# Weight splits of two experts moved into the phase before, and a product kept in PSUM, in a four-stage transformer kernel

## The reference, cut to what matters

```python
scores = softmax(x2d @ wg_router.T)                  # 32 experts
topk_w, topk_idx = top_k(scores, 6)
xe = zeros((E, C, D)).at[flat_idx, safe_pos].add(x_rep)   # C = 384 slots for an expert
g, u = xe @ w_gate, xe @ w_up                        # width 176
ye = (silu(g) * u) @ w_down
y = sum over the 6 choices of ye * topk_w
sh = silu(x2d @ ws_gate) * (x2d @ ws_up) @ ws_down   # shared experts, width 352
out = x + y + sh                                     # x2d is the layer-normed x
```

## Time and profile before

| | us |
|---|---|
| three runs: median (lowest to highest) | 1120.21 (1117.7 to 1127.51) |
| profiled execution, its own time | 1119.49 |
| its span | 1117.7 |
| mean granted TensorE clock | 0.975 |
| PE busy | 1031.1 (92%) |
| DVE busy | 758.2 (68%) |
| ACT busy | 600.6 (54%) |
| POOL busy | 563.0 (50%) |

### The profile page before, as it was taken

One profiled execution on the slowest core, in us unless ns is written; L12 is line 12 of the kernel. 1 busy time (PEld: TensorE's weight loads), 2 busy tenths in 40 slices (PEclk: granted clock), 3 DMA queues, 4 the chain that ended last, 5 costly groups with the idle time before them and its releaser, 6 DMA issues. The chain is left out here.

```text
span 1117.7 us, 16700 instructions
## 1 busy us (share of the span) xinstructions
PE 1031.1 (92%) x6084; PEld 865.8 (77%) x6084; DVE 758.2 (68%) x1344; ACT 600.6 (54%) x1060; POOL 563.0 (50%) x411
## 2 busy tenths in 40 slices
PE   5899999999999999999998899996978887999992
PEld 4788888888888888888886676654765686999992
DVE  4877764777557776567775644467688755888877
ACT  3566663666536666456662423333523245888871
POOL 1574633756236563365540357762224777655553
PEclk9999999999999999999999999999998898999996
DMA  7510340003701991000001146631300366777766
GB/s 202 50 34 1 48 47 1 24 1 44 52 1 38 230 216 45 1 1 1 1 1 39 44 161 204 218 132 57 109 2 5 108 224 231 232 231 227 234 206 225
DMA packets 45343, 109.79 MB, mean 98 GB/s; under 512 B 8487, under 2 KB 25525, under 8 KB 43216
## 3 DMA queue, kind: packets, MB, share of 16 engines
q1 hardware_dynamic: 38352, 95.46, 32.5%
q0 software_dynamic: 6912, 13.30, 3.2%
HBM read 94.27 MB, written 41.29 MB: 121 GB/s over the span
## 5 line engine op out<-in xcount | busy, mean ns | idle before, releaser
L460 POOL TENSOR_TENSOR at_prob<-at_prob,at_inv_sum 128x1024 f32<-128x1024 f32 x128 | 243.8, 1907 | 272.7 <-DVE at_inv_sum L678 272.7
L641 ACT ACTIVATE at_pt_h<-ps 128x512 fp32r<-128x512 f32 x256 | 139.2, 596 | 139.4 <-PE ps L566 139.3
L729 DVE TENSOR_TENSOR at_pt_l<-ps,at_pt_h 128x512 fp32r<-128x512 f32 x256 | 164.4, 684 | 60.9 <-ACT at_pt_h L641 60.9
L718 DVE TENSOR_REDUCE at_neg_max<-ps 128x1 f32<-128x1024 f32 x128 | 154.6, 1208 | 35.8 <-PE ps L41 35.4
L608 ACT ACTIVATE at_prob<-ps,at_neg_max 128x1024 f32<-128x1024 f32 x128 | 143.7, 1123 | 15.3 <-DVE at_neg_max L718 15.3
L566 PE MATMUL ps<-ident,at_prob 128*128 128x128 f32 x1024 | 133.4, 273 | 5.1 <-POOL at_prob L460 3.9
L566 PEld LDWEIGHTS ps<-ident,at_prob 128*128 128x128 f32 x1024 | 118.9, 140 | 23.0 <-POOL at_prob L460 4.7
L2111 POOL DMA_INDIRECT lines<-f_y,f_x_raw x96 | 96.0, 1000 | 72.1 <-ACT f_y L2027 42.6
L39 PE MATMUL ps<-at_k_h,at_q_h 128*128 128x512 f32 x256 | 108.4, 423 | 0.0
L39 PE MATMUL ps<-at_pt_h,at_v_h 128*128 128x512 f32 x256 | 100.3, 392 | 0.0
L40 PE MATMUL ps<-at_k_l,at_q_h 128*128 128x512 f32 x256 | 100.2, 391 | 0.0
(11 more groups left out here) (318 smaller groups left out, 2456.5 us busy)
## 6 DMA issues: line engine op xcount, KB each, us to landing
e_raw<-in_we SPq DMA_DIRECT2D x32, 624.0 KB, 4.3
f_cw_row<-cw SPq DMA_DIRECT2D x32, 512.0 KB, 4.2
slots<-in_empty SPq DMA_DIRECT2D x4, 3456.0 KB, 41.9
f_x_raw<-slots SPq DMA_DIRECT2D x32, 432.0 KB, 4.9
lines<-in_empty SPq DMA_DIRECT2D x3, 2048.0 KB, 33.3
f_e_raw<-in_we SPq DMA_DIRECT2D x32, 128.0 KB, 2.5
at_wq_raw<-in_wq SPq DMA_DIRECT2D x4, 512.0 KB, 3.6
at_wo_raw<-in_wo SPq DMA_DIRECT2D x4, 512.0 KB, 3.5
```

What stands on the lines that cost most here:

```text
L460: nc.gpsimd.tensor_tensor(prob[:, t % RING, :], prob[:, t % RING, :], inv_sum[:, t:t + 1].broadcast_to([P, T]), ALU.mult).then_inc(normed, 1)
L641: nc.scalar.activation(pt_h[:, e[1] % PT, :], turned(e[1]), ACT.Copy).then_inc(pt_high, 1)
L718: nc.vector.tensor_reduce(neg_max[:, t:t + 1], slot(n, start), AX.XY, ALU.max, negate=True).then_inc(maxed, 1)
L729: nc.vector.tensor_tensor(pt_l[:, e[1] % PT, :], turned(e[1]), pt_h[:, e[1] % PT, :].bitcast(F32), ALU.subtract).then_inc(pt_split, 1)
```

## The change

1. The tiles `e_h` and `e_l` and their two semaphores are made outside the silu experts' phase, so that the linear attention can write them (`e_h1`, `e_l1`, `e_high1`, `e_split1`).
2. ScalarE's copies for experts 0 and 1 move into the linear attention, ahead of `square(6)`. GpSimd's subtractions for experts 0 and 1 move there too, behind a wait for the last state update and ahead of `shared_l`.
3. In the head of the silu experts ScalarE and GpSimd split expert 2 instead of 0 and 1. The expert loop no longer splits expert 2.
4. SyncE's order becomes weights 3, weights 4, slots 0, slots 1, slots 2, weights 5, slots 3, weights 6, and so on: `load_weights(n + 3)` stands behind `load_slots(n)`, where `load_weights(n + 2)` stood.
5. The shared experts' product is written back over the up projection in PSUM; `s_act` is gone. `s_h` and `s_l` are made from PSUM. The up projection alternates between banks 4, 5 and banks 6, 7.

```diff
@@ linear attention, GpSimd @@
+                pool.wait_ge(state_done, TT)
+                for n in range(AHEAD1):
+                    pool.wait_ge(net.e_high1, n + 1)
+                    nc.gpsimd.tensor_tensor(net.e_l1[:, n, :], net.e_raw1[:, n, :], net.e_h1[:, n, :].bitcast(F32),
+                                            ALU.subtract).then_inc(net.e_split1, 1)
                 pool.wait_ge(chain, NB * ROOT)
@@ linear attention, ScalarE @@
+                for n in range(AHEAD1):
+                    act_e.wait_ge(net.e_loaded1[n], 16)
+                    nc.scalar.activation(net.e_h1[:, n, :], net.e_raw1[:, n, :], ACT.Copy).then_inc(net.e_high1, 1)
                 for i in range(TT - 2, TT):
                     square(i)
@@ constants @@
+WRING1 = 4
+AHEAD1 = 2
@@ silu experts, SyncE @@
+                for n in range(AHEAD1):
+                    load_weights(n + RAW)
                 load_slots(0)
                 load_slots(1)
-                for n in range(1, EXP1):
-                    if n > 1:
-                        load_slots(n)
-                    if n + RAW - 1 < EXP1:
-                        load_weights(n + RAW - 1)
+                for n in range(2, EXP1):
+                    load_slots(n)
+                    if n + RAW < EXP1:
+                        load_weights(n + RAW)
@@ TensorE @@
+        def s_banks(k):
+            return slice(4 + 2 * (k % 2), 6 + 2 * (k % 2))
                     project(2, k, rows, SG)
-                    if k:
-                        pe.wait_ge(timed, k)
-                        project(4, k, rows, SU)
-                    else:
+                    if k == 0:
                         ranks(1)
                         norm.wait_parts(pe)
-                        project(4, k, rows, SU)
+                    if k >= 2:
+                        pe.wait_ge(act_split, k - 1)
+                    project(s_banks(k).start, k, rows, SU)
@@ ScalarE @@
-                for n in range(2):
-                    high_weights(n)
+                high_weights(AHEAD1)
-                    nc.scalar.activation(s_h[0:rows, k, :], s_act[0:rows, k % 2, :], ACT.Copy).then_inc(act_high, 1)
+                    nc.scalar.activation(blocks(s_h[0:rows, k, :]), ps[0:rows, s_banks(k), :], ACT.Copy).then_inc(act_high, 1)
-                    if n + 2 < EXP1:
+                    if AHEAD1 < n + 2 < EXP1:
                         high_weights(n + 2)
@@ GpSimd @@
-                for n in range(2):
-                    pool.wait_ge(e_high, n + 1)
-                    nc.gpsimd.tensor_tensor(e_l[:, n % WRING, :], e_raw[:, n % RAW, :], e_h[:, n % WRING, :].bitcast(F32),
-                                            ALU.subtract).then_inc(e_split, 1)
+                pool.wait_ge(e_high, AHEAD1 + 1)
+                nc.gpsimd.tensor_tensor(e_l[:, AHEAD1, :], e_raw[:, AHEAD1, :], e_h[:, AHEAD1, :].bitcast(F32),
+                                        ALU.subtract).then_inc(e_split, 1)
@@ VectorE @@
-                    if k >= 2:
-                        dve.wait_ge(act_split, k - 1)
-                    nc.vector.tensor_tensor(blocks(s_act[0:rows, k % 2, :]), ps[0:rows, 4:6, :], blocks(s_silu[0:rows, k % 2, :]),
+                    nc.vector.tensor_tensor(ps[0:rows, s_banks(k), :], ps[0:rows, s_banks(k), :], blocks(s_silu[0:rows, k % 2, :]),
                                             ALU.mult).then_inc(timed, 1)
-                    nc.vector.tensor_tensor(s_l[0:rows, k, :], s_act[0:rows, k % 2, :], s_h[0:rows, k, :].bitcast(F32),
-                                            ALU.subtract).then_inc(act_split, 1)
+                    nc.vector.tensor_tensor(blocks(s_l[0:rows, k, :]), ps[0:rows, s_banks(k), :],
+                                            blocks(s_h[0:rows, k, :].bitcast(F32)), ALU.subtract).then_inc(act_split, 1)
-                    if n == 1:
-                        dve.wait_ge(e_split, 2)
-                    if 2 <= n + 1 < EXP1:
+                    if n == AHEAD1:
+                        dve.wait_ge(e_split, AHEAD1 + 1)
+                    if AHEAD1 < n + 1 < EXP1:
                         low_weights(n + 1)
```

More of the change, by code:

```diff
@@ L1693, in silu_experts_phase @@
 def silu_experts_phase(nc, net, out):
-    WRING, XRING, YRING = 4, 7, 6
+    WRING, XRING, YRING = WRING1, 7, 6
     SENT = 8 - TOP1
@@ L1712, in silu_experts_phase @@
         row = sb("row", [P, TT, ROW1])
-        e_h, e_l = sb("e_h", [P, WRING, W1E], F32R), sb("e_l", [P, WRING, W1E], F32R)
+        e_h, e_l = net.e_h1, net.e_l1
         x_raw = sb("x_raw", [P, XRING, SLOTS, ROW1])
@@ L1725, in silu_experts_phase @@
         e_raw, e_loaded, RAW = net.e_raw1, net.e_loaded1, RAW1E
-        s_silu, s_act = only_early("s_silu", [P, 2, T]), only_early("s_act", [P, 2, T])
+        s_silu = only_early("s_silu", [P, 2, T])
         s_h, s_l = only_early("s_h", [P, SH1, T], F32R), only_early("s_l", [P, SH1, T], F32R)
@@ L1754, in silu_experts_phase @@
         x_loaded = [sem(f"x_loaded{r}") for r in range(XRING)]
-        e_high, e_split = sem("e_high"), sem("e_split")
+        e_high, e_split = net.e_high1, net.e_split1
         x_turned, x_high, x_split = sem("x_turned"), sem("x_high"), sem("x_split")
@@ L2305, in program @@
         net.e_raw1 = sb("e_raw1", [P, RAW1E, W1E])
+        net.e_h1, net.e_l1 = sb("e_h1", [P, WRING1, W1E], F32R), sb("e_l1", [P, WRING1, W1E], F32R)
+        net.e_high1, net.e_split1 = (ctx.enter_context(nc.semaphore(n)) for n in ("e_high1", "e_split1"))
         net.shared1_high, net.shared1_split = (ctx.enter_context(nc.semaphore(n)) for n in ("shared1_high", "shared1_split"))
```

## The result

The changed kernel takes 1144.64 us (median of 4 runs, 1137.29 to 1145.85) where the kernel before takes 1121.74 (4 runs): a ratio of 1.0186, 95% interval 1.0142 to 1.0229. It is slower, by about 21 to 23 us. The forecast was 1138, with a range of 1129 to 1148.

What follows compares the result with a forecast made beforehand. The prediction took the loop to be bound by TensorE. The turn of expert 29 moves from 1072.38 to 945.2 + 11 x 13.27 = 1091.2, so +18.8 on the profiled 1119.49: 1138 us, range 1129 to 1148.

Steps and rivals of the forecast that it cites:

- The deciding step: SyncE's queue in the expert loop: gathered rows released one expert later, 3.24 us before use against a median 5.3 us transfer.
- the round: Expert loop: two iterations take 7.52 + 0.41 + 5.3 + 0.04 = 13.27 us instead of 11.18, eleven times.
- the landing: Expert loop: time for gathered rows to arrive after issue, taken as the median 5.3 us, mean allowed 4.9 to 5.8.
- The head: Silu experts before the loop: 6.0 us gained (4 to 7), all eaten by the turn of expert 7.
- The copy: Head: VectorE's 128x24 copy, held by GpSimd's subtractions, drops from 2.38 to 0.20 us, gaining 2.18.
- the 1.25 for expert 2's low parts: Head: the dispatch at 910.67, which took 2.23 us beside expert 2's low parts, becomes 1.25 us shorter.
- The 2.75 beside `s_low`: Head: three GpSimd dispatches beside `s_low` return to 0.98 us, saving 1.04 + 1.00 + 0.71.
- The size in the loop: From the turn of expert 7 at 945.2 to that of 29 at 1091.2: 11 rounds of 13.27 us.
- the fall of the clock: Rival for the whole loop: TensorE's idling lowers its clock; at half clock 1225 us in all; chance 0.03.
- The tail: What follows the turn of expert 29 was claimed to keep its length.
- Costed at nothing: Moved splits hide in ScalarE's and GpSimd's idle time; the product written to PSUM costs at most 0.1 us each.
- The Trainium skill's fit: DMA estimate: rows land in 3.0 us alone, 4.1 behind weights, giving the landings-of-about-4.1 rival, 1124 us, chance 0.07.

Runs made afterwards that it cites:

- Experiment 2: Kernel before with SyncE's new order alone; weights still split in the head, product still in SBUF: 1147.68 us, ratio 1.0257.
- experiment 1: Changed kernel with slots n + 1 again ahead of weights n + 3 in SyncE's queue: 1116.39 us, ratio to before 0.9965; second series 1116.0 us, 0.9956.
- experiments 3 and 4: For 3 see experiment 3; 4: changed kernel loading only half of each expert's weights from expert 6 on, order as changed: 1132.72 us, ratio to before 1.0114.
- experiment 3: Changed kernel, same wait for expert n's low parts, but slots n + 1 issued ahead of weights n + 3: 1118.8 us, ratio to before 0.9989.
- experiment 5: Changed kernel with gathered rows again one expert further ahead and the shared experts' product back in SBUF: 1120.42 us, ratio to before 0.9988.
- experiment 6: Kernel before with the shared experts' product in PSUM alone, head splits and SyncE's order as before: 1120.83 us, ratio 1.001.

## Why the prediction was right

**The deciding step, SyncE's order**, held in every part. The turn before which the wait sits, the round and its terms are in the chain after: 1004.56 to 1009.86 is landing plus 0.04, 1009.86 to 1017.47 is 7.61 (forecast 7.52), 0.38 for the issue. Experiment 2 shows that the order alone makes the loss, experiment 1 that nothing else in the change does, experiments 3 and 4 that its size goes by the landing.

**The head** held nearly to the figure. The copy: 0.18 for 2.38. Dispatches began 2.7 us earlier (868.01 to 865.28), of which 0.5 is the block's earlier start. The turn of 4 came at 923.90 (forecast 924.4), that of 5 at 933.83 (933.6), that of 7 at 944.64 (945.2). The sum behind it was mis-sized in one term: 3.4 us less from the first to the fortieth dispatch (55.2 to 51.8) instead of 4.0. Nothing was got of the 1.25 for expert 2's low parts: the dispatch at 913.24 met those of expert 3 instead and took 2.25. The 2.75 beside `s_low` were got in full. The rest of the 3.4 is luck: another dispatch, that of 917.22, had been long before (1.65), was not in the forecast, and has no counterpart after.

**The size in the loop** was short by 3.8 us. The forecast had 146.0 for eleven rounds; from 944.64 to 1094.48 are 149.84, or 13.62 a round. The mis-sized term is the landing. The forecast took the median of 5.3 for each; the ten on the chain of the loop have a mean of 5.5, which makes 2.0. Eight of them landed in 4.7 to 5.3, and the rounds in which the chain comes straight back took 12.75 to 13.55, as forecast. Two took 15.1 and 15.4, with loads that landed in 7.1 and 7.4 us. Such loads are not new. One mark of the first is a slow issue by SyncE, and before the change there were slow issues too (from the two timelines, before and after):

```profile
1013.04 1.91 SPq L1853 DMA_DIRECT2D f_x_raw<-slots  x1
...
1017.85 1.54 SPq L1866 DMA_DIRECT2D f_x_raw<-slots  x1
```

The load of 1013.04 landed in 6.0 us, and one of 1029.86, issued in 1.64, in 6.8; neither held anyone, as there were 8.8 us of slack. What makes an issue slow no run shows. Behind the turn of 1024.99, ahead of which TensorE had stood still for 2.99 us, the granted clock fell: it is 0.52 from 1024.99 to 1031.30, transposes took 1.54 instead of 0.87, and the next turn came 8.6 us later. This iteration and a later one, both of which the chain crosses on TensorE, took 14.4 together where the forecast has 13.3 for two. I had given the fall of the clock 0.03 as a state of the whole loop; it came as an episode. In the window 949 to 1072 the clock is still 0.97. The last 0.7 of the 3.8 are the other terms of the round, 8.04 on average for 7.97.

**The tail** kept its length only nearly: from the turn of 29 to the end 47.5 us, before 45.3. The turn of 30 came 7.4 behind that of 29, at a lowered clock (0.65 from 1094.48 to 1099.20; three loads of rows had gone out together, the first landing in 7.4 us). The account closes: the forecast's 18.8, less 0.6 for the better head, plus 3.8 for the loop and 2.2 for the tail is 24.2, and the spans differ by 24.3. But for the 0.6 the misses have one sign, so the forecast of 1138 was not saved by errors that cancel; it was 6.6 short of 1144.64.

**Costed at nothing**: the moved splits were hidden (ScalarE 828.85 to 831.2, GpSimd 833.12 to 838.8, VectorE's roots from 839.07 on at their 0.23 to 0.29). The product written to PSUM took 1.22 to 1.23, no more than the 1.21 to 1.23 to SBUF.

**The Trainium skill's fit** for a DMA ("DMA: Bandwidth & Descriptors", section "Anatomy of one DMA — SWDGE (gpsimd) path", made on DMAs that GpSimd issues) gives, as an estimate, 4.1 us for the rows behind the weights and 3.0 for the rows alone. For these loads, which SyncE issues, the traces do not agree: the median is 5.0 with the weights just ahead, and 3.5 with the weights behind them in experiment 3.

What stays open: the moves alone (experiment 5, 0.9988) and the PSUM product alone (experiment 6, 1.001) show no gain outside their intervals, the two together 4 to 5 us. Each of the two figures is uncertain by some 2 us either way, so it is not shown that the sum is more than its parts; nor is it shown how the 4 to 5 us divide between the moves and the product.

## What to carry to other kernels

In a queue that is served in order, a wait is paid by whatever stands behind it. When a load is moved in such a list, count for each entry how many iterations ahead of its use it is now released, and set that lead against the time to landing with what goes out in front of it. Here the lead went from 8.8 to 3.2 us against a landing of 5. The queue's waits for the low parts of the weights add up to 100.9 us before and to 100.0 in experiment 3, and do little or no harm in either. The same 24 waits with the entries behind them shifted by one cost 2%, and come to 141.4 us because the loop is longer. The sum of the waits is no measure of what they cost; the slack of what stands behind them is.

## What the runs showed of the hardware

One thing I had not expected is how much the same kernel's head moves from run to run. Experiment 1's kernel began its dispatches at 864.19 us in one profiled execution and at 873.81 in the other, spans 1112.4 and 1119.8. The same two windows of both, the faster one first, with the granted clock behind the busy times:

```profile
615.00:650.00 35.00, 30.05 (x169) 25.60 (x169) 21.49 (x102) 15.66 (x19) 11.66 (x6) 0.95 0.26 97
...
780.00:850.00 70.00, 60.08 (x655) 45.17 (x656) 53.52 (x111) 26.38 (x54) 25.51 (x26) 0.98 0.12 44
```

```profile
615.00:650.00 35.00, 30.42 (x138) 25.96 (x138) 21.03 (x101) 14.32 (x17) 9.97 (x6) 0.79 0.22 69
...
780.00:850.00 70.00, 59.99 (x627) 44.45 (x626) 48.93 (x92) 30.93 (x62) 23.75 (x24) 0.88 0.13 44
```

In the second, TensorE was granted its lower level for longer (a clock of 0.79 and 0.88, against 0.95 and 0.98), in stages where it is busy about 86% of the time in both. That is the size of the effects that experiments 5 and 6 looked for, and a reason why single profiles can't settle them. That the clock made the whole difference between the two was not tested.
